# A gated cross-attention and mixture network on one core: summed softmax denominators, one-pass causal scores and masked-token experts

## The reference, cut to what matters

```python
q, k, v = (einsum('bsd,hed->bhse', embed, W) + b)           # 16 heads of 8 features
att = where(tril, q @ k.T, 0.0) / sqrt(128)                  # not -inf: later keys score 0
att = softmax(att); x = (att @ v) reshaped to (tokens, 128)
probs = softmax(x @ Wsw.T + bsw); routes = argmax(probs); route_probs = max(probs)
pos = running count of tokens with this route; kept = pos < capacity    # int(1.2 * 2048 / 8)
y = where(kept, x @ We[route].T + be[route], x) * route_probs           # 8 experts, one per token
out = layernorm(y + embed)
```

## Time and profile before

| | |
|---|---|
| median of three runs | 2015.8 us (2008.92, 2015.8, 2047.99) |
| the profiled execution | 2023.89 us |
| its span, from first to last instruction | 2022.1 us |
| busy: TensorE, VectorE, ScalarE, GpSimd | 83%, 47%, 35%, 7% of the span |
| mean granted clock of TensorE | 0.862 of full |

### The profile page before, as it was taken

How to read it: one execution, slowest core, us unless ns; L and a number is a source line. 1 busy time by engine, 2 the same in 40 slices (tenths; PEclk the granted TensorE clock), 3 DMA queues, 4 the chain that set the end, 5 groups by cost and what they waited for, 6 DMA issues and landing times.

```text
span 2022.1 us, 23678 instructions
## 1 busy us (share of the span) xinstructions
PE 1687.4 (83%) x9546; PEld 757.0 (37%) x9552; DVE 950.3 (47%) x2022; ACT 710.7 (35%) x1255; POOL 131.7 (7%) x183
## 2 busy tenths in 40 slices
PE   5738999889798878987549999898898879988577
PEld 2223322332343525722124332332443425623365
DVE  4474662432566363234664663333576273246412
ACT  2332455313344204242342554323254114233133
POOL 0000111000011100000000111000011000002132
PEclk8768899978899878996777999978799788888788
DMA  4000000000000100000000000000000100003141
GB/s 175 0 0 0 1 1 1 0 1 1 0 2 1 42 0 0 1 1 2 0 0 0 1 1 1 0 1 1 0 2 1 42 0 1 1 1 73 48 134 63
DMA packets 18112, 30.50 MB, mean 15 GB/s; under 512 B 4640, under 2 KB 12640, under 8 KB 17104
## 3 DMA queue, kind: packets, MB, share of 16 engines
q1 hardware_dynamic: 16752, 26.35, 4.0%
q0 software_dynamic: 1248, 2.59, 0.4%
HBM read 23.75 MB, written 5.19 MB: 14 GB/s over the span
## 4 chain that ended last, share of the span: by engine, by line
PE 73%; DVE 15%; ACT 7%; issue 3%; DMA 1%; POOL 1%; SPq 0%; POOLq 0%; ACTq 0%; DVEq 0%
PE ps L702 11%; PE ps L755 5%; PE ps L724 5%; PE ps L774 4%; PE ps L618 4%; PE ps L561 3%; PE ps L1114 3%; PE ps L1126 3%; PE ps L840 3%; PE ps L832 2%; PE ps L593 2%; PE ps L627 2%; PE ps L639 2%; PE ps L726 2%; ACT big L1365 2%
## 5 line engine op out<-in xcount | busy, mean ns | idle before, releaser
L1414 ACT ACTIVATE big<-ps 128x512 f32<-128x512 f32 (+3 forms) x512 | 239.4, 515 | 250.4 <-PE ps L726 208.6
L702 PE MATMUL ps<-pp,qT 32*128 32x512 f32 (+3 forms) x1024 | 301.2, 627 | 19.6 <-DVE pt L2015 9.0
L724 PE MATMUL ps<-qT,pp 32*128 32x512 f32 (+3 forms) x1024 | 282.3, 572 | 0.0
L1746 DVE TENSOR_REDUCE peak<-ps 128x1 f32<-128x512 f32 x256 | 165.1, 685 | 121.9 <-PE ps L702 121.8
L702 PEld LDWEIGHTS ps<-pp,qT 32*128 32x128 f32 x1024 | 119.4, 205 | 155.9 <-DVE peak L1746 66.4
L1743 DVE CUSTOM_DVE_ANT_0 ps<-ps,cst 128x128 f32<-128x128 f32 (+3 forms) x256 | 133.7, 557 | 82.9 <-PE ps L702 81.2
L1365 ACT ACTIVATE big<-ps 77x1024 f32<-77x1024 f32 x96 | 94.5, 1018 | 125.6 <-PE ps L618 125.2
L1692 DVE TENSOR_REDUCE small<-ps 128x8 f32<-128x616 f32 x96 | 74.4, 797 | 127.1 <-PE ps L593 64.0
L1346 ACT ACTIVATE sq<-ps 128x512 f32<-128x512 f32 x52 | 31.0, 597 | 292.4 <-PE ps L561 292.4
L755 PE MATMUL ps<-big,cst 128*32 128x512 f32 (+3 forms) x1024 | 117.5, 531 | 0.0
L726 PE MATMUL ps<-spare,minus 32*128 32x512 bf16 (+3 forms) x512 | 112.7, 340 | 0.0
(11 more groups left out here) (429 smaller groups left out, 2521.2 us busy)
## 6 DMA issues: line engine op xcount, KB each, us to landing
big<-in_w SPq DMA_DIRECT2D x23, 256.0 KB
pt<-in_l2w SPq DMA_DIRECT2D x2, 2048.0 KB, 7.5
w_l<-in_l SPq DMA_DIRECT2D x1, 3086.0 KB, 18.3
pp<-in_w SPq DMA_DIRECT2D x1, 2048.0 KB, 9.7
cst<-in_const SPq DMA_DIRECT2D x1, 1549.0 KB, 7.2
big<-by_expert SPq DMA_DIRECT2D x23, 66.0 KB, 1.9
by_expert<-cst SPq DMA_DIRECT2D x1, 1472.0 KB, 16.0
w_l<-in_l SPq DMA_DIRECT2D x1, 1218.0 KB, 9.3
```

The lines of the kernel that those rows point to most:

```text
L702: pe.matmul(rbank(x)[:, 0:hi], qT[at, u, 0 if causal else k, 128 * i:128 * i + 128], keyT(u, k)[at, 0:hi], start=True, stop=True, tile_pos ...
L724: pe.matmul(tbank(y)[:, lo:512], keyT(u, k)[at, 128 * j:128 * j + 128], qT[at, u, 0 if causal else k, lo:512], start=True, stop=False, til ...
L1414: A(prob(m)[:, TURN_OF[g], lo:512], tbank(tplace(m, g, causal))[:, lo:512], ACT.Exp)\
L1746: v.tensor_reduce(top, rbank(ring(p, c)), AX.X, ALU.max).then_inc(*VECTOR.did(tag, "max", p, c))
```

## The change

Cross attention with `dh` = 8: no `sums`. The masked value tile's zero columns of two other heads are filled with ones (`ones_beside`, on GpSimd), so that a product with the exponentials gives values for one half of the rows and denominators in the other. Two pairs of k are added up in two banks. `heads` picks one denominator per head, `head_inverse` takes the reciprocal of 64 columns and copies it out eight wide, `inverses` turns it back, `joined` puts the halves together and `divided` multiplies.

The causal attention becomes `attend_past`. Its q has four masked versions. The maximum is added to q's unused rows (`raised`), with -1 in the keys' matching rows (constant `below`), so the column scores need no second product. The mask of the row scores is a bf16 product into the same bank (`diagonals`), and maxima cover two banks at a time with a plain reduction. The row scores' order is 1, 0, 3, 2 (`ktile_past`), which gives row and column scores of one step the same width. The ones beside the values replace `sums`. The exponential of a zero score is taken from the 64 maxima (`e0`) and spread by products (`spread_out`). Only q and k of u = 0 are waited for before the first score; the other parts are made inside the loop.

The experts: for n = 8u + e, `chosen` spreads row e of the transposed one-hot routes over 128 partitions, VectorE multiplies the tokens by it (`only_of`), and `expert` multiplies the masked 512 tokens by We[e], all eight adding up in one bank. Gates are spread and applied to the sum (`gates`, `passed`, `mixed`). Counts use bf16.

```diff
+    t["below"] = -(row % 32 // 2 == (np.arange(4)[None, :] + 2) % 4 * 4).astype(f)
...
+            def ones_beside(tag, free):
+                for u in U:
+                    if free:
+                        pool.wait_ge(*TENSOR[free, u])
+                    for h in (0, 1):
+                        ins = pool.tensor_copy(vx[:, u, 256 * h:256 * h + 256], K["col8"][0:KC, 256 - 256 * h:512 - 256 * h])
+                    ins.then_inc(*POOL.did(tag, "ones", u))
...
+                def heads(u, hf):
+                    x = 34 + u
+                    if hf == 0:
+                        free_late(x)
+                    pe.wait_ge(*SCALAR[tag, "kept", u, hf])
+                    to = PSB[cbank(x)][:, 0:64].rearrange("p (i c k) -> p i c k", i=4, c=4)
+                    source = (xn if hf == 0 else sq)[:, u, :]
+                    for i in range(4):
+                        mm = pe.matmul(to[:, i, :, 2 * hf:2 * hf + 2], source[:, 128 * i:128 * i + 128],
+                                       eighths[:, :, 1 - hf, :], start=True, stop=True, skip_group_check=True)
+                    mm.then_inc(*TENSOR.did(tag, "heads", u, hf))
+                def free_late(x):
+                    pe.wait_ge(*SCALAR[tag, "exp", 1, x - 29])
...
+                def inverses(u):
+                    pe.wait_ge(*VECTOR[tag, "inv", u])
+                    for i in range(4):
+                        mm = pe.matmul(PSB[cbank(34 + u) + 1][:, 128 * i:128 * i + 128], rs[:, u, 128 * i:128 * i + 128], ident,
+                                       start=True, stop=True)
+                    mm.then_inc(*TENSOR.did(tag, "inverses", u))
...
+                def rowscore(p, c):
+                    Q, i = p // 4, ktile_past(p)
+                    u, k, h = Q // 4, Q % 4, c // 2
+                    x = pplace(p, h)
+                    last = pbefore(x)
+                    if c % 2 == 0 and last:
+                        pe.wait_ge(*VECTOR["l1f", "max" if len(last) == 2 else "raised", *last])
+                    if p == 16 and c == 0:
+                        pe.wait_ge(*SCALAR["l1f q", 1])
+                        pe.wait_ge(*SCALAR["l1f k", 1])
+                    at = slice(32 * c, 32 * c + 32)
+                    hi = 128 * (i + 1)
+                    pe.matmul(PSB[pbank(x) + c % 2][:, 0:hi], qT[at, u, k, 128 * i:128 * i + 128], keyT(u, k)[at, 0:hi],
+                              start=True, stop=False, tile_position=(32 * c, 0))
+                def diagonals(p, h):
+                    x, lo = pplace(p, h), 128 * ktile_past(p)
+                    for b in (0, 1):
+                        mm = pe.matmul(PSB[pbank(x) + b][:, lo:lo + 128], identb[:], beyond[:], start=False, stop=True)
+                    mm.then_inc(*TENSOR.did("l1f", "R", p, h))
...
+                    lo = 128 * j
+                    y = tplace(n, g)
+                    if tbefore(y):
+                        pe.wait_ge(*SCALAR["l1f", "exp", tbefore(y)[0], tbefore(y)[1]])
+                    else:
+                        pe.wait_ge(*(SCALAR["l1f", "suffix", 0], SCALAR["l1f q", 1], SCALAR["l1f k", 1])[y])
+                    if n % 4 == 0 and g == 0:
+                        pe.wait_ge(*VECTOR["l1f", "raised", Q])
+                    at = slice(32 * c, 32 * c + 32)
+                    pe.matmul(tbank(y)[:, lo:512], keyT(u, k)[at, 128 * j:128 * j + 128], qT[at, u, k, lo:512], start=True,
+                              stop=True, tile_position=(32 * c, 0)).then_inc(*TENSOR.did("l1f", "T", n, g))
...
+                        if g == 2 and m >= 2:
+                            values(m - 2)
+                        if m + 6 < 32:
+                            rowscore(m + 6, g)
+                        if m < 32:
+                            colscore(m, g)
+                        if m + 6 < 32 and g % 2:
+                            diagonals(m + 6, g // 2)
+                    if m == 28:
+                        pe.wait_ge(*VECTOR["l1f", "max", 31, 1])
+                        spread_out("e0", 0, 1)
+                    if m == 29:
+                        spread_out("e0", 1, 2)
+                        heads(0, 0)
+                        heads(0, 1)
+                    if m == 31:
+                        spread_out("inv", 0, 4)
+                    if m == 32:
+                        heads(1, 0)
+                heads(1, 1)
+                logits(0)
+                spread_out("inv", 1, 2)
             def linear(tag, w, src, ready, rows=None):
...
+                def chosen(n):
+                    u, e = n // E1, n % E1
+                    if e == 0:
+                        pe.wait_ge(*SCALAR["l1f hotT", u])
+                    if n >= 3:
+                        pe.wait_ge(*VECTOR["l1f only", n - 3])
+                    pe.matmul(PSB[3 + n % 3], identb[0:E1, e:e + 1].to_broadcast([E1, 128]), hotT(u), start=True, stop=True)\
+                        .then_inc(*TENSOR.did("l1f chosen", n))
+                def expert(n):
+                    u, e = n // E1, n % E1
+                    pe.wait_ge(*VECTOR["l1f only", n])
+                    mm = pe.matmul(lin(u), w["We"][:, 128 * e:128 * e + 128], only(n), start=e == 0, stop=False)
+                    if e == E1 - 1:
+                        pe.wait_ge(*SCALAR["l1f hotT wide", u])
+                        mm = pe.matmul(lin(u), w["be"][0:E1, :], cwT(u, E1), start=False, stop=True)
...
+                turned_hot(0)
+                for n in range(3):
+                    chosen(n)
+                for n in range(2 * E1):
+                    expert(n)
+                    if n + 3 < 2 * E1:
+                        if n + 3 == E1:
+                            turned_hot(1)
+                        chosen(n + 3)
+                    if n == 1:
+                        logits(1)
+                    if n in (6, 12):
+                        gates(n // 12, True)
+                    if n in (8, 14):
+                        gates(n // 14, False)
...
+                def joined(u, hf):
+                    v.wait_ge(*SCALAR[tag, "kept", u, hf])
+                    if hf == 0:
+                        v.tensor_scalar(part[:, u, :], xn[:, u, :], K["half"][:, 0:1], None, ALU.mult)\
+                            .then_inc(*VECTOR.did(tag, "joined", u, hf))
+                    else:
+                        v.wait_ge(*VECTOR[tag, "joined", u, 0])
+                        v.scalar_tensor_tensor(part[:, u, :], sq[:, u, :], K["half"][:, 1:2], part[:, u, :], ALU.mult, ALU.add)\
+                            .then_inc(*VECTOR.did(tag, "joined", u, hf))
+                def head_inverse(u):
+                    v.wait_ge(*TENSOR[tag, "heads", u, 1])
+                    chain(v.reciprocal(sm(u, 0, 64), PSB[cbank(34 + u)][:, 0:64]))
+                    v.tensor_copy(rs[:, u, :].rearrange("p (n r) -> p n r", r=8), sm(u, 0, 64).unsqueeze(2).to_broadcast([128, 64, 8]))\
+                        .then_inc(*VECTOR.did(tag, "inv", u))
...
+                def maxima(p):
+                    Q, i = p // 4, ktile_past(p)
+                    u, k, hi = Q // 4, Q % 4, 128 * (i + 1)
+                    for h in (0, 1):
+                        b = pbank(pplace(p, h))
+                        v.wait_ge(*TENSOR["l1f", "R", p, h])
+                        v.tensor_reduce(crest[:, u, i, 2 * h:2 * h + 2, k], ps[:, b:b + 2, 0:hi], AX.X, ALU.max)\
+                            .then_inc(*VECTOR.did("l1f", "max", p, h))
...
+                def raised(Q):
+                    q = qT[:, Q // 4, Q % 4, :]
+                    v.wait_ge(*TENSOR["l1f", "turned", Q])
+                    if Q == 4:
+                        v.wait_ge(*SCALAR["l1f q", 1])
+                    v.tensor_tensor(q, q, PSB[pbank(pturned(Q))].bitcast(BF16)[:, 0:512], ALU.add)\
+                        .then_inc(*VECTOR.did("l1f", "raised", Q))
...
+                def only_of(n):
+                    v.wait_ge(*TENSOR["l1f chosen", n])
...
+                        v.wait_ge(*TENSOR["l1f expert", n - 4])
+                    v.tensor_tensor(only(n), x2[:, n // E1, :], PSB[3 + n % 3], ALU.mult).then_inc(*VECTOR.did("l1f only", n))
...
+                attend_past(token_values, route)
+                for n in range(2 * E1):
+                    only_of(n)
+                    if n == 2:
+                        route(1)
+                    elif n in (4, 9):
+                        gates(n // 9)
+                    elif n == 11:
+                        passed(0)
+                    elif n == 13:
+                        mixed(0)
+                passed(1)
+                mixed(1)
```

718 lines of the change are left out of this document (422 added, 296 removed).

## The result

The changed kernel takes 1954.72 us in the median of four executions (1932.59 to 1982.08), the kernel before 2012.36 beside it (2003.18 to 2047.99). The ratio is 0.969 with an interval of 0.960 to 0.978. Medians are of all executions; ratios leave disturbed ones out on either side. The forecast was 1888, with a range up to 1945: the kernel is faster, by 58 us instead of 128.

A forecast was written before the change was run, and what follows sets the result against it. TensorE was taken to bound the kernel, with 73% of the chain of waits (VectorE 15%). Terms of -14, -7, -19, +1 and -24 gave -63 a turn, -126 for both, -128 with smaller constants: 2015.8 to 1888 us, range 1865 to 1910, reaching to 1850 and 1945.

The forecast's parts named there:

- The cross attentions: Two cross attention stages a turn: removed sums give 7 us each, -14 us a turn (bounds -18 and -4).
- the ends cancel: Cross attentions' end: new end about 5.7 us against 4.9, offset by the projection taking half of its 2.06 us.
- Before the loop: Causal attention before its loop: shorter first wait and cheaper maxima, 28 us to 21, -7 us a turn (-13 to -1).
- The loop: Causal attention's loop: four steps 12.1 us instead of 13.98, stalls gone, 98.5 to 79.6, -19 us a turn (-29 to -7).
- Rival A: Causal loop no faster per step, column-score banks and switches keeping 14 us for four steps: 1912 us, chance 0.17.
- twice my price for the changes: Causal loop: tiling-mode changes at twice 0.1 us each make four steps 13.7 us, gain 9 instead of 19, total 1908.
- Its end: End of the causal loop: sums and second products go, fp32 groups and a wait come, +1 us a turn (-3 to +4).
- The experts: Experts stage: 61.5 us falls to 37.4, mostly TensorE's 25.0 us program, -24 us a turn (-29 to -2).
- Low clock at first: 3.0: Experts' start: 3.0 us charged for TensorE running at the low clock, within the stage's 37.4 us.
- rival B: Experts run at 1.2 GHz, 22 us a turn lost: 1932 us, chance 0.12.
- Rival C: Without sums the clock never leaves 1.2 GHz in the causal attention and stays low through the experts: 2088 us, chance 0.04.
- Rival D: Cross attentions gain nothing: exponentials set the pace and the longer end eats the rest, 14 us a turn: 1916, chance 0.09.

The follow-up runs named there:

- b_cross_only: The kernel before with the change in its four cross attentions alone: 2042.26 us against 2013.07, ratio 1.008.
- a_fill: The changed kernel plus two unread bf16 products of 448 columns ahead of each `heads` group: 1932.43 us, ratio 0.963 to the kernel before.
- b_cross_fill: The kernel before with the change in its cross attentions alone, plus unread wide products at those stages' start and ahead of `heads`: 1983.59 us, ratio 0.980.
- e0_fill_all: The changed kernel with `e0`'s exponential a step sooner and unread wide products ahead of `heads`, at the cross attentions' start and in the experts: 1896.73 us.
- a_again: The changed kernel once more, nothing edited, for a second profile: 1957.24 us, ratio 0.978 to the kernel before.
- e0_fill_start: The changed kernel with `e0`'s exponential a step sooner and unread wide products ahead of `heads` and at the cross attentions' start: 1890.02 us, ratio 0.936.
- a_e0_sooner: The changed kernel with the exponential of u = 1's 64 maxima behind step 28's exponentials instead of step 29's: 1969.36 us.

## Why the prediction was wrong

**The cross attentions: -14 a turn forecast, +1.3 measured.** This is the largest part of what is missing, 30 us over both turns. The failed step is "With TensorE busy in the gap the projection should take half, so the ends cancel." TensorE was busy, with `heads` and `inverses`, and the clock fell within them all the same: `inverses` 2.05 us, the second `heads` 1.72, and 10.7 us from the last `values` to the projection's end where the kernel before had 7.1. I had priced the groups by the row of the logits at the high clock and taken being busy for what brings the clock up. In layer 3's stage of turn two, which ran at 0.83, this is most of the miss: up to the first column score it takes the 8.5 us of before, the middle is 5.0 us shorter where 7 were forecast, and the end 3.6 longer where nothing was. Of the middle, 0.9 us are `heads(0, ...)`, which were to be free: they end at 1717.7, and the exponentials that they were to hide behind at 1716.8. The rest of the error is a low clock in the middle of other stages: at 0.56 to 0.60 a stage takes 63.5 to 66.6 us (in the change itself and in b_cross_only). The content of the end was sized right: 5.7 us and half a projection are 6.7, and with the clock held a_fill has 7.6, 0.8 of it fillers. That b_cross_fill's 29.5 us come so near to the 28 is in part luck, since its fillers also give back clock that the kernel before had lacked.

**Before the loop: -7 forecast, -7.0 measured** from the norm's first product to the loop, -5.8 (27.9 to 22.1) as the prediction counted, from the last product ahead of the first score. The first score waits 0.36 us instead of 4.50:

```profile
1387.06 0.70 PE L881 MATMUL ps<-pp,qT 32*128 32x256 f32 x4 [0.36 <-ACT pp L1739]
```

**The loop: -19 forecast, -17.9 measured** (98.5 to 80.6). `values` of the steps with 512 columns mark four steps each:

```profile
1465.57 1.07 PE L932 MATMUL ps<-big,pt 128*32 128x512 f32 x8
1478.01 1.06 PE L932 MATMUL ps<-big,pt 128*32 128x512 f32 x8
1490.56 1.06 PE L932 MATMUL ps<-big,pt 128*32 128x512 f32 x8 [0.27 <-ACT part L1646]
```

12.44 and 12.55 us, against 12.1 forecast and 13.98 before. Rival A falls. The stalls for `taken(0)` and the reciprocals are gone, and the clock is 1.00 throughout. The Trainium skill ("TensorEngine Tiling (Array Packing)", Key Properties) charges a drain for each change of tiling mode. At twice my price for the changes four steps would have been 13.7 us; the trace stands near my 0.1 for each.

**Its end: +1 forecast, +11.9 measured.** The failed step is the same one, in "Four or five groups of four fp32 products come (about 5), and at step 29 TensorE waits for ScalarE's `e0`": the clock was not thought of. The 14 us from 1503 to 1517 at 1.2 GHz hold 7 us of it. Moving `e0` gave 3.3, and wide products with it 6.8 in all: 105.2 us for 112.0. Part of the rest is a miscount: six groups of four fp32 products stand ahead of the last `values` and a seventh ahead of the logits, where "four or five" were counted.

**The experts: -24 forecast, -20.7 measured** (61.5 to 40.8; from the logits on it is 19.4). The failed step is the term "Low clock at first: 3.0": TensorE ran at 1.2 GHz from 1521 to 1541. The forecast's 37.4 count from the last `values`, 2.0 us ahead of the logits; so counted the change took 42.8 us (1518.8 to 1561.6). Turn one of e0_fill_all, at clock 1.00, took 36.7 so counted, with 2.1 of fillers: 34.6, where the forecast without its 3.0 has 34.4. So the content was sized right, and the low clock cost 8.2 us instead of 3.0. So rival B, the experts at 1.2 GHz, was right for half of the stage. The doubling is plain in `expert`:

```profile
1533.95 2.05 PE L1242 MATMUL ps<-big,w_l1f 128*128 128x512 f32 x2
...
1551.89 1.13 PE L1242 MATMUL ps<-big,w_l1f 128*128 128x512 f32 x2
```

**The sum.** By the profiles the changed stages gave 65 us where 126 were forecast: 30.6 are missing in the cross attentions, 22 at the loop's end, 7 in the experts, 2 in the loop. The medians differ by 58, with the typical execution of the changed kernel at a clock of 0.858 (the middle of its nine) and that of the kernel before at 0.868 (the middle of the seven beside a_again). Rival C named the clock, but put its loss into the causal attention's start and loop, where there was none. Rival D named the cross attentions, and its 14 us a turn are nearly what is missing there, but with the exponentials as its reason; ScalarE has 7% of the chain, and b_cross_fill shows that the exponentials leave 47 us possible.

## What to carry to other kernels

Price a new program at the clock that it will itself leave behind, not at the clock of the row that it replaces: here the products that followed groups of 8-column products cost double for some 10 us and more, although TensorE had not stood still. Where a stretch of waits and such small products is short, a few wide products that nobody reads can be worth more than the work they add (e0_fill_start: ratio 0.936 for 0.969); put them ahead of the narrow group and into the wait before it, and test with a narrow control of the same type. And compare stages, not totals, when stages that no edit touches differ by 11 us between two executions of one kernel.

## What the runs showed of the hardware

- TensorE was busy without a gap from 1494 to 1504 (a_e0_sooner), and the granted clock fell from 1.00 to 0.50 within the second group of fp32 products of 8 columns. With two bf16 products of 448 columns ahead of each group it stayed at 1.00; with two fp32 products of 8 columns in the same places it fell (0.71 over the stretch). The Trainium skill ("TensorE: Matmul & The Clock Gate", Part 1) ties the gate to how busy TensorE has been recently. In these rows being busy by the records did not hold it. The clock also fell, from 1.00 to 0.71 over 1.4 us, right behind a wait of 1.66 us with no such product before it (a_fill, `spread_out` at 1504.4).
- Dense work does not bring it back at once: from 1527 to 1541 `expert` products of 512 columns ran at 1.2 GHz, and layer 3's cross attention of turn one stayed there for most of 40 us (820 to 860, clock 0.51), TensorE being busy for 33.9 of the 35 us from 825 on.
- One stage of one kernel has a small set of times: layer 1's second cross attention took 66.7, 71.8 or 78.0 to 79.7 us in these profiles with the same instructions. What draws one of them was not settled.
